# Idle sums moved from the key blocks into the down product, and a second attention with rings of tiles, a bias row by TensorE and another order on each engine

## The chip, the core and the metric

The kernel runs on one core of one Trainium2 chip. The metric is the device time of one execution in microseconds (us), as the median of a few runs.

## What is computed

The input is 32 tiles of 128 tokens with 256 columns. Two layers follow, each an attention over a context and then a feed-forward part, all with residuals:

```
x = x + attention_L0(layernorm(x), ctx, mask)      # 16 heads of 16
x = x + ffn_L0(layernorm(x))                       # 256 -> 768 -> 256, below
x = x + attention_L1(layernorm(x), ctx)            # 16 heads of 64, below
x = x + experts_L1(layernorm(x))                   # 8 experts, 256 -> 1024 -> 256, below

ffn_L0(x):                       # act_qdq rounds to 16 bits; its scale is the maximum of |tensor| over all 32 tiles
  x = act_qdq(x)
  up, gate = act_qdq(x @ dequant(w_up).T), act_qdq(x @ dequant(w_gate).T)
  o = act_qdq(act_qdq(gate * round16(sigmoid(gate))) * up)
  return o @ dequant(w_down).T
attention_L1(q, ctx):
  Q, K, V = q @ Wq + bq, ctx @ Wk + bk, ctx @ Wv + bv
  out = softmax(Q K.T / sqrt(64)) V @ Wo + bo + q
  return layernorm(out) * gamma + beta
experts_L1(x):
  for i in range(8):             # the token's mask is 1 where expert i is its best, else 0
    out += relu((x * mask) @ W1[i] + b1[i]) @ W2[i] + b2[i]
```

For a token that is not an expert's own, the expert still adds relu(b1[i]) @ W2[i] + b2[i], the same row for all tokens. The kernel computes relu(b1) @ W2 once for each expert; these eight rows are the idle sums.

## The kernel before

The program is four functions, one behind the other: attention0, feed_forward0, attention1 and experts. In each, every engine has its own queue of instructions, written out by hand; semaphores tie them. PE is TensorE, DVE VectorE, ACT ScalarE, POOL GpSimd, and SP is SyncE, which issues most of the DMAs; loads of contexts and of weight halves for the key and value blocks are issued on POOL's queue. A number that TensorE needs at more than its rounding is split into a high and a low part, and a product is three matmuls (PARTS). inside(b, first, last) is true where step b lies in that range.

**feed_forward0.** The up and gate products run over 8 chunks of 512 tokens. Then comes the block stage: the 64 key blocks and 64 value blocks of the second attention, 128x512 each, six matmuls a block, which TensorE makes while ScalarE and VectorE do the elementwise part of the FFN, 12 units of 2048 columns. PSUM has seven banks for the blocks and an eighth for the idle sums. ScalarE copies each block out (copy_block), and SP stores it (store_block). ScalarE's queue goes: four blocks; for each unit sigmoid(u) (two passes) and four blocks; copy_idle; three blocks; then, once VectorE and GpSimd have found the scale of the SiLU, quantise_silu for the units with three or four blocks between.

The idle sums are 16 pieces: piece (g, f) takes 128 of the 1024 hidden rows for four experts, as four matmuls of 256 columns onto 32 partitions each. load_w2(i) loads its W2 rows, four DMAs of 128 KB into the one buffer w2, and waits for the piece before to be done. TensorE's queue has idle_sums behind every third block, from the third on. Down stage: 32 tiles, four to a chunk; TensorE makes 18 matmuls of 256 columns a tile (down), ScalarE splits off the high part of the next chunk (high_inner), VectorE adds the residual x1; SP loads x1 and stores x2.

**attention1.** All engines run steps b = FIRST = -4 to LAST = NB + 3 = 35, with Python's unrolled steps at the ends and a hardware loop of four steps between. Step b works on several tiles at once: it turns xn of tile b + 4 (turn_x), projects queries of the pair ahead (queries; from step -2 on), scores and exponentials of tile b in four groups of four heads, half of them in each of two score calls (scores, maxima, exponentials, divide), turns the probabilities (transposes, copy_probT), weights the values (weighted), makes the output product of tile b - 1 (output: 24 matmuls of 256 columns), the output norm of b - 2 (normalise_output), and norm, turning and routing logits of b - 3 and b - 4 (normalise_routed, turn_z, logits_of, route). ps_score (two groups), ps_probT (two), ps_out and ps_proj are PSUM buffers of their own; turned x, turned z, logits and the output product take turns in one bank, ps_aux. Each tile of x2 is loaded twice, into x2_early (four tiles; for xn) and x2_late (four; for the residual and beta). GpSimd makes xn + bo again from x2_late in three passes and x2 + beta in a fourth. Ahead of the first queries TensorE multiplies bv by Wo (bias_through_output, 128 equal rows), which VectorE adds to bo.

The maximum of a group is turned into the bias of the exponential by a second VectorE instruction:

```
dve.tensor_reduce(row_max[:, n, :], ps_score[:, n % 2], AX_X, ALU.max).then_inc(max_done, 1)
dve.wait_ge(max_done, m)
dve.tensor_scalar(shift[:, n, :], row_max[:, n, :], -float(KD) ** -0.5, None, ALU.mult)
...
last = act.activation(prob[:, n, j, :], ps_score[:, n % 2, j, :], ACT.Exp, scale=float(KD) ** -0.5,
                      bias=shift[:, n, j:j + 1], accum_out=row_sum[:, n, j:j + 1])
```

## Time and profile before

| | |
|---|---|
| median of 3 runs | 1651.63 us |
| lowest, highest | 1647.52, 1653.64 us |
| profiled execution, its span | 1649.6 us, 1647.8 us |
| mean granted TensorE clock | 0.92 |
| attention0 | 0 to about 290 us |
| up and gate products | about 290 to 444 us, TensorE busy 140.88 of 154 |
| block stage | 444 to about 701 us |
| down product | about 704 to 775 us |
| end of down, head of attention1 | 775 to 803 us, TensorE busy 12.72 of 28, DMA share 0.72 |
| attention1 | 803 to 1344.8 us |
| experts | 1344.8 to 1647.8 us, TensorE busy 274.92 of 303 |

The span is what the profile shows of the profiled execution, from its first instruction to its last; the execution's own time is 1.8 us longer. An engine's busy time is the sum of its instructions. The granted clock is a share of TensorE's full 2.4 GHz, 0.5 being its lower level of 1.2 GHz. Waiting shows as the gap before an instruction, with the one that ended it.

### The profile page before, as it was taken

What the parts mean: (1) busy time and instruction counts of PE and PEld (TensorE: products, weight loads), DVE (VectorE), ACT (ScalarE), POOL (GpSimd) and SP (SyncE); (2) the same over time, 40 slices, a digit from 0 to 9 for tenths busy, and PEclk for the clock granted to TensorE, in tenths of its full rate; (3) what the DMA queues carried; (4) which work ended last, traced back from release to release, by engine and by line L of the source; (5) the groups of instructions that cost most, each with busy time, mean ns of one, the idle gap of its engine ahead of it and who ended that gap; (6) DMA issues with size and microseconds to landing.
All of it is one profiled execution on the core that took longest, in us unless ns stands there. A gap on an engine that the chain in (4) does not pass through costs nothing. (4 is left out here: it accounts for less than half of the span.)

```text
span 1647.8 us, 35334 instructions
## 1 busy us (share of the span) xinstructions
PE 1389.3 (84%) x11229; PEld 1184.0 (72%) x11229; DVE 1183.1 (72%) x2102; ACT 1047.2 (64%) x2716; POOL 431.9 (26%) x735
## 2 busy tenths in 40 slices
PE   5788888898867689998788888898888867999997
PEld 3455555686744468898677778787777757999996
DVE  6688777887645569086477777777777766888885
ACT  4677778574466656463566666666666625888885
POOL 5444443000000001002123222323232313444443
PEclk9999999899988889999799989989998878999998
DMA  7311010472366778743413232232323135511110
GB/s 225 100 31 35 29 35 28 144 280 90 113 195 199 231 240 268 261 139 109 169 65 114 93 103 77 83 121 76 102 76 120 38 129 210 195 45 54 54 47 9
DMA packets 106773, 194.91 MB, mean 118 GB/s; under 512 B 13474, under 2 KB 72893, under 8 KB 100288
## 3 DMA queue, kind: packets, MB, share of 16 engines
q1 hardware_dynamic: 96320, 160.13, 29.0%
q0 software_dynamic: 10176, 33.57, 6.8%
q8 instruction: 47, 0.77, 0.2%
q14 instruction: 38, 0.31, 0.1%
q10 hardware_dynamic: 192, 0.13, 0.0%
HBM read 128.49 MB, written 68.03 MB: 119 GB/s over the span
## 5 line engine op out<-in xcount | busy, mean ns | idle before, releaser
L1996 ACT ACTIVATE c_w_raw<-c_ps_score,c_shift 128x128 f32<-128x128 f32 x512 | 184.0, 393 | 172.3 <-DVE c_shift L1872 135.9
L2373 PE MATMUL d_ps_hT<-d_zT,d_w_tile 128*128 128x128 f32 x1248 | 148.5, 278 | 1.6 <-DVE d_zT L2480 1.6
L2373 PEld LDWEIGHTS d_ps_hT<-d_zT,d_w_tile 128*128 128x128 f32 x1248 | 145.3, 195 | 2.3 <-DVE d_zT L2480 2.3
L2386 PE MATMUL d_ps_y<-d_w_parts,d_hT 128*128 128x256 f32 x936 | 121.8, 287 | 1.8 <-DVE d_res L2511 1.8
L1996 ACT ACTIVATION_READ_ACCUMULATOR c_w_raw<-c_ps_score,c_shift 128x1 f32 x512 | 118.8, 232 | 0.0
L2386 PEld LDWEIGHTS d_ps_y<-d_w_parts,d_hT 128*128 128x128 f32 x936 | 114.6, 191 | 2.0 <-DVE d_res L2511 2.0
L581 ACT ACTIVATE a_probT<-a_ps_probT 128x512 f32<-128x512 f32 x128 | 71.1, 623 | 66.2 <-PE a_ps_probT L368 66.2
L459 DVE TENSOR_REDUCE a_row_max<-a_ps_score 128x8 f32<-128x1024 f32 x64 | 78.0, 1218 | 48.6 <-PE a_ps_score L357 48.6
L2546 ACT ACTIVATE d_h<-d_ps_hT,d_b1T 128x128 f32<-128x128 f32 x312 | 88.7, 367 | 37.8 <-PE d_ps_hT L2373 37.8
L2499 DVE TENSOR_TENSOR d_w_parts<-d_w,d_w_parts 128x1024 fp32r<-128x1024 f32 x78 | 95.2, 1221 | 23.7 <-ACT d_w_parts L2558 23.7
L1754 PE MATMUL c_ps_proj<-c_xnT,c_wq 128*128 128x256 f32 x768 | 105.9, 288 | 0.0
L1801 PE MATMUL c_ps_aux<-c_wo,c_attnT 128*128 128x256 f32 x768 | 99.3, 285 | 3.0 <-DVE c_attnT L1892 2.9
L1724 PE MATMUL c_ps_score<-c_kT,c_qT 64*128 64x128 f32 x1024 | 92.6, 332 | 8.5 <-ACT c_w_raw L1996 6.9
L1754 PEld LDWEIGHTS c_ps_proj<-c_xnT,c_wq 128*128 128x128 f32 x768 | 94.4, 191 | 3.8 <-issue 0.2
L1801 PEld LDWEIGHTS c_ps_aux<-c_wo,c_attnT 128*128 128x128 f32 x768 | 93.6, 191 | 4.8 <-issue 3.4
L1724 PEld LDWEIGHTS c_ps_score<-c_kT,c_qT 64*128 64x128 f32 x1024 | 79.2, 232 | 24.8 <-ACT c_w_raw L1996 12.7
L1869 DVE TENSOR_REDUCE c_row_max<-c_ps_score 128x4 f32<-128x512 f32 x128 | 87.4, 683 | 7.7 <-PE c_ps_score L1724 7.5
L1699 POOL TENSOR_TENSOR c_var_o<-c_mv_o,c_eps 128x1 f32<-128x1 f32 x32 | 6.8, 213 | 327.0 <-DVE c_mv_o L1915 327.0
L1878 DVE RECIPROCAL c_inv_sum<-c_row_sum 128x4 f32<-128x4 f32 x128 | 22.4, 175 | 97.1 <-ACT c_w_raw L1996 97.1
L1880 DVE TENSOR_TENSOR c_w_raw<-c_w_raw,c_inv_sum 128x512 f32<-128x512 f32 x128 | 88.6, 692 | 4.5 <-DVE c_inv_sum L1878 0.2
L1043 PE MATMUL b_ps<-b_ctx_high,b_w_parts 128*128 128x512 f32 x256 | 91.9, 431 | 0.0
L2558 ACT ACTIVATE d_w_parts<-d_w 128x1024 fp32r x78 | 80.4, 1054 | 13.7 <-PE d_ps_y L2386 12.6
(299 smaller groups left out, 3731.3 us busy)
## 6 DMA issues: line engine op xcount, KB each, us to landing
keys_scratch<-b_out SPq DMA_DIRECT2D x64, 256.0 KB, 3.6
values_scratch<-b_out SPq DMA_DIRECT2D x64, 256.0 KB, 3.6
c_kT<-keys_scratch SPq DMA_DIRECT2D x16, 1024.0 KB, 6.4
d_w<-w_in SPq DMA_DIRECT2D x16, 1024.0 KB, 8.0
split_scratch<-b_split SPq DMA_DIRECT2D x12, 1024.0 KB, 4.7
c_v_more<-values_scratch SPq DMA_DIRECT2D x24, 512.0 KB, 3.9
b_ctx_high<-split_scratch POOLq DMA_DIRECT2D x16, 512.0 KB, 6.1
b_ctx_low<-split_scratch POOLq DMA_DIRECT2D x16, 512.0 KB, 7.5
```

What stands on the lines that cost most here:

```text
L1043: last = pe.matmul(ps[:, bank(n), :], w_parts[:, h, a, k, column:column + P], ctx_parts[c % 2][b][:, k, :], start=(j == 0), stop=(j == ND ...
L1724: last = pe.matmul(ps_score[:, r, j, :], qT[rows, s, blk, tok], kT[rows, s, blk, tok], start=True, stop=True)
L1754: last = pe.matmul(ps_proj[:, j, h * PT:(h + 1) * PT], weights[:, a, k, blk * P:(blk + 1) * P], src[:, c, k, :], start=(n == 0), stop=(n = ...
L1801: last = pe.matmul(ps_aux[:, 0:D], attnT[:, s, a, blk, :], wo[:, c, blk, :], start=(n == 0), stop=(n == BLKS * len(PARTS) - 1))
L1869: dve.tensor_reduce(row_max[:, n, :], ps_score[:, n % 2], AX_X, ALU.max).then_inc(max_done, 1)
L1880: dve.tensor_tensor(prob[:, n], prob[:, n], inv_sum[:, n, :].unsqueeze(2).to_broadcast([P, HB, P]), ALU.mult).then_inc(prob_ready, 1)
L1996: last = act.activation(prob[:, n, j, :], ps_score[:, n % 2, j, :], ACT.Exp, scale=float(KD) ** -0.5, bias=shift[:, n, j:j + 1], accum_out ...
L2373: last = pe.matmul(ps_hT[:, f, :], w1_tile[:, half, k, n * P:(n + 1) * P], zT[:, s, k, :], start=(k == 0), stop=(k == ND - 1))
L2386: last = pe.matmul(ps_y[:, 0:D], hT[:, s, a, f, :], w2_parts[:, half, b, n, :], start=(f == 0 and (a, b) == PARTS[0]), stop=(f == FB - 1 a ...
L2499: dve.tensor_tensor(w2_parts[:, half, 1], w2[:, e, half * FB // 2:(half + 1) * FB // 2, :], w2_parts[:, half, 0].bitcast(F32), ALU.subtrac ...
L2546: act.activation(h[:, f, :], ps_hT[:, f, :], ACT.Relu, bias=b1T[:, e, f:f + 1]).then_inc(h_ready, 1)
L2558: act.activation(w2_parts[:, half, 0], w2[:, e, half * FB // 2:(half + 1) * FB // 2, :], ACT.Copy)\
```

## The change

In feed_forward0 the idle sums leave the block stage: TensorE makes one piece behind every second tile of the down product (odd n; 16 pieces, 32 tiles). w2 becomes a ring of three buffers, with a semaphore each, in memory that yT, upT and gateT held before; SP issues load_w2(t // 2) at even t among its loads of x1 and stores of x2. ScalarE copies the sums out (copy_idle) at the end of its down loop, and they are stored ahead of the last x2. The down product's loops on SP and TensorE are written out.

In attention1 one ring of eight x2 tiles takes the place of two of four, and each tile is loaded once; xn has a ring of eight too and is itself the residual, so that GpSimd only adds beta. bo (with bv Wo) comes in as a matmul of two rows of ones by the two parts of bo, ahead of the output product and into the same bank; bias_through_output makes two rows, in step 0 instead of step -2. The queries are scaled by 1/8 as they are copied (their bias bq ahead of the loop), the maximum is written negated and is itself the exponential's bias. normalise_output has two VectorE passes of two operations instead of three passes. The hardware loop takes eight steps, twice. The order within a step changes on PE, DVE and ACT, and the loads at the head change order. In experts, one small ScalarE activation (at_tile) stands ahead of some copies instead of behind them.

The core of the diff, with sixteen columns of indentation cut. It leaves out names, semaphores, the same edits where they repeat, TensorE's order within a step (shown below), and the new bias_parts, which are five VectorE instructions on two rows of 256 that split bo into its two parts.

```diff
-w2 = x_space[:, 0:4 * D].rearrange("p (e d) -> p e d", d=D)
-idle = x_space[:, 0:BANK].rearrange("p (g d) -> p g d", g=2)
-down_int = x_space[:, BANK:BANK + NF * D // 4].bitcast(I16)
+w2 = [raw_at(f"w2_{n}", [P, 4, D], offset)
+for n, offset in enumerate((address["yT"] + 4 * (2 * T - ITEM), address["upT"], address["gateT"]))]
+idle = out2[:].rearrange("p (g d) -> p g d", g=2)
...
+    if t >= 4:
         sp.wait_ge(x2_ready, t - 3)
     sp.dma_start(x1_sb[:, s, :], x1_dram[t]).then_inc(x1_loaded[s], 16)
-    if inside(t, 3, NB - 1):
+    if t >= 3:
         store(t - 3, (s + 1) % 4)
+    if t % 2 == 0:
+        load_w2(t // 2)
...
-    if i >= 1:
-        sp.wait_ge(idle_part, i)
+    if i >= 3:
+        sp.wait_ge(idle_part, i - 2)
     for e in range(4):
-        sp.dma_start(w2[:, e, :], w2_dram[4 * g + e][:, f, :]).then_inc(w2_loaded, 16)
+        sp.dma_start(w2[i % 3][:, e, :], w2_dram[4 * g + e][:, f, :]).then_inc(w2_loaded[i % 3], 16)
...
-    if n % IDLE_EVERY == IDLE_EVERY - 1 and w2_pieces < 2 * FB:
-        load_w2(w2_pieces)
-        w2_pieces += 1
-    if n == KEYS:
-        sp.wait_ge(idle_ready, 1)
-        for e in range(4):
-            sp.dma_start(idle_dram[e:NE:4].unsqueeze(0), idle[32 * e:32 * e + 1]).then_inc(idle_stored, 16)
 sp.wait_ge(block_done, ALL)
 sp.dma_start(wq_raw[:], wq_dram).then_inc(wq_loaded, 16)
-sp.wait_ge(idle_stored, 64)
...
-for t in range(4):
-    step(t, t)
-with sp.Fori(1, NB // 4) as i:
-    for s in range(4):
-        step(4 * i + s, s)
-for t in range(NB - 3, NB):
-    store(t, t % 4)
+for t in range(NB):
+    step(t, t % 4)
+store(NB - 3, (NB - 3) % 4)
+store(NB - 2, (NB - 2) % 4)
+sp.wait_ge(idle_ready, 1)
+for e in range(4):
+    sp.dma_start(idle_dram[e:NE:4].unsqueeze(0), idle[32 * e:32 * e + 1]).then_inc(idle_stored, 16)
+store(NB - 1, (NB - 1) % 4)
 sp.wait_ge(wq_loaded, 16)
+sp.wait_ge(idle_stored, 64)
...
-    pe.wait_ge(w2_loaded, 64 * (i + 1))
+    pe.wait_ge(w2_loaded[i % 3], 64 * (i // 3 + 1))
...
             pe.wait_ge(x2_ready, n - TILES + 1)
         for j, (f, (a, b)) in enumerate(product(range(NF), PARTS)):
             last = pe.matmul(ps[:, t, 0:D], inner[:, s, a, f, t * P:(t + 1) * P],
                              down_parts[b][:, f, :], start=(j == 0), stop=(j == NF * len(PARTS) - 1))
         last.then_inc(down_done, 1)
-for c in range(2):
-    down(c, c)
-with pe.Fori(1, NC // 2) as i:
-    for s in range(2):
-        down(2 * i + s, s)
+        if n == 1:
+            pe.wait_ge(relu_b1_ready, 1)
+        if n % 2 == 1:
+            idle_sums(n // 2)
+for c in range(NC):
+    down(c, c % 2)
...
-copy_idle()
 copy_blocks(done, done + 3)
 done += 3
...
-pool.wait_ge(bo_added, 1)
-def residuals(t, u, i):
-    s = u % 2
-    pool.wait_ge(late_loaded[u], 16 * uses(t, None if i is None else i + 1))
...
-    pool.tensor_tensor(xn_bo[:, s, :], xn_bo[:, s, :], bo[:], ALU.add).then_inc(xn_bo_ready, 1)
-    pool.tensor_tensor(x2_late[:, u, :], x2_late[:, u, :], beta[:], ALU.add).then_inc(x2_beta_ready, 1)
+pool.wait_ge(bias_loaded, 16 * N_BIAS)
+def residual(t, w):
+    pool.wait_ge(xn_ready, t + 1)
+    pool.tensor_tensor(x2[:, w, :], x2[:, w, :], beta[:], ALU.add).then_inc(x2_beta_ready, 1)
...
+    if inside(b, 4, NB):
+        bank_after_logits(b)
+    else:
         pe.wait_ge(xnT_ready, b + 5)
-    else:
-        bank_after_logits(b)
-    pe.wait_ge(attnT_ready, 2 * t + 2)
     if isinstance(b, int) and b == 1:
         pe.wait_ge(w_split, 2)
+        pe.wait_ge(bo_ready, 1)
+        pe.wait_ge(ones_ready, 1)
+    pe.matmul(ps_aux[:, 0:D], two_ones[:], bo_parts[:], start=True, stop=False)
+    pe.wait_ge(attnT_ready, 2 * t + 2)
...
+def normalise(t, w, uses_now):
+    dve.wait_ge(x2_loaded[w], 16 * uses_now)
+    if inside(t, RING, NB - 1):
+        dve.wait_ge(xnT_done, t - RING + 1)
+        dve.wait_ge(proj_ready, t - RING + 1)
+    dve.tensor_scalar(xn[:, w, :], x2[:, w, :], mv2[:, t, 0:1], rstd2[:, bass.ds(t, 1)],
                       ALU.subtract, ALU.mult).then_inc(xn_ready, 1)
 def maxima(b, n):
-    m = NU * b + n + 1
     dve.wait_ge(scores_done, 2 * b + n // 2 + 1)
-    dve.tensor_reduce(row_max[:, n, :], ps_score[:, n % 2], AX_X, ALU.max).then_inc(max_done, 1)
-    dve.wait_ge(max_done, m)
-    dve.tensor_scalar(shift[:, n, :], row_max[:, n, :], -float(KD) ** -0.5, None, ALU.mult)\
-       .then_inc(shift_ready, 1)
+    dve.tensor_reduce(neg_max[:, n, :], ps_score[:, n % 2], AX_X, ALU.max, negate=True).then_inc(max_done, 1)
...
-    dve.wait_ge(xn_bo_ready, t + 1)
-    dve.tensor_tensor(proj[:, s, :], ps_aux[:, 0:D], xn_bo[:, s, :], ALU.add).then_inc(proj_ready, 1)
+    dve.tensor_tensor(proj[:, s, :], ps_aux[:, 0:D], xn[:, w, :], ALU.add).then_inc(proj_ready, 1)
...
+    dve.wait_ge(mv_o_done, t + 1)
+    dve.scalar_tensor_tensor(proj[:, s, :], proj[:, s, :], mv_o[:, s, 0:1], gamma[:],
+                             ALU.subtract, ALU.mult).then_inc(scaled_done, 1)
     dve.wait_ge(rstd_o_done, t + 1)
-    dve.tensor_scalar(proj[:, s, :], proj[:, s, :], mv_o[:, s, 0:1], rstd_o[:, s, :],
-                      ALU.subtract, ALU.mult).then_inc(normed_done, 1)
-    dve.wait_ge(normed_done, t + 1)
-    dve.tensor_tensor(proj[:, s, :], proj[:, s, :], gamma[:], ALU.mult).then_inc(scaled_done, 1)
     dve.wait_ge(scaled_done, t + 1)
     dve.wait_ge(x2_beta_ready, t + 1)
     if inside(t, 4, NB - 1):
         dve.wait_ge(zx_stored[u], 16 * (uses(t, i) - 1))
-    dve.tensor_tensor(x3[:, u, :], proj[:, s, :], x2_late[:, u, :], ALU.add).then_inc(x3_ready, 1)
+    dve.scalar_tensor_tensor(x3[:, u, :], proj[:, s, :], rstd_o[:, s, :], x2[:, w, :],
+                             ALU.mult, ALU.add).then_inc(x3_ready, 1)
...
-    if isinstance(b, int) and b == projects[0]:
-        dve.wait_ge(bias_loaded, 16 * N_BIAS)
-        dve.wait_ge(bias_turned, 1)
-        dve.tensor_tensor(bo[:], bo[:], ps_out[:, 0:2, :].rearrange("p h k -> p (h k)"), ALU.add).then_inc(bo_added, 1)
-    if inside(b, FIRST, NB - 5):
-        normalise(b + 4, u, None if i is None else i + 2)
     here, back = inside(b, 0, NB - 1), inside(b, 1, NB)
-    if back:
-        split_attn(b - 1, (u + 1) % 2, 0)
+    if not inside(b, 0, LAST) and inside(b, FIRST, NB - 5):
+        normalise(b + 4, (w + 4) % RING, 1)
     if here:
         maxima(b, 0)
         maxima(b, 1)
-    if inside(b, 2, NB + 1):
-        normalise_output(b - 2, (u + 2) % 4, turn[2])
-    if inside(b, 4, NB + 3):
-        route(b - 4)
-    if here:
-        divide(b, 0)
-        divide(b, 1)
+    if back:
+        split_attn(b - 1, (u + 1) % 2, 0)
     if isinstance(b, int) and (b, 0) in split_at:
         rest_of_weights(split_at[b, 0])
     if inside(b, FIRST, NB - 5):
         split_x(b, u)
+    if isinstance(b, int) and (b, 1) in split_at:
+        rest_of_weights(split_at[b, 1])
+    if inside(b, 2, NB + 1):
+        normalise_output(b - 2, (u + 2) % 4, (w - 2) % RING, turn[2])
+    if here:
+        divide(b, 0)
+        divide(b, 1)
+    if back:
+        split_attn(b - 1, (u + 1) % 2, 1)
+    if inside(b, 4, NB + 3):
+        route(b - 4)
     if inside(b, 3, NB + 2):
         normalise_routed(b - 3, (u + 1) % 4, turn[3])
-    if back:
-        split_attn(b - 1, (u + 1) % 2, 1)
-    if isinstance(b, int) and (b, 1) in split_at:
-        rest_of_weights(split_at[b, 1])
     if here:
         maxima(b, 2)
         maxima(b, 3)
+    if isinstance(b, int) and b == 0:
+        bias_parts()
+    if here:
         divide(b, 2)
+    if inside(b, -1, NB - 6):
+        normalise(b + 5, (w + 5) % RING, ring_uses(b, w, i, 5))
+    if back:
+        add_residual(b - 1, (u + 1) % 2, (w - 1) % RING)
+    if here:
         divide(b, 3)
     if back:
-        add_residual(b - 1, (u + 1) % 2)
-    if isinstance(b, int) and (b, 3) in split_at:
-        rest_of_weights(split_at[b, 3])
...
-def step(b, u, i):
+def step(b, w, i):
+    u = w % 4
     if isinstance(b, int) and b == projects[0]:
-        act.wait_ge(bias_loaded, 16 * N_BIAS)
+        act.wait_ge(bq_scaled, 1)
     here, back = inside(b, 0, NB - 1), inside(b, 1, NB)
     if back:
         copy_attn(b - 1, (u + 1) % 2, 0)
+    if inside(b, FIRST, NB - 5):
+        copy_x(b, u)
     if here:
         exponentials(b, 0)
-    if inside(b, 4, NB + 3):
-        copy_z(b - 4)
-    copy_queries(b, u, 0)
     if back:
         copy_probT(b - 1, 2)
         copy_probT(b - 1, 3)
     if here:
         exponentials(b, 1)
-    copy_queries(b, u, 1)
-    if isinstance(b, int) and split_at.get((b, 0)):
-        round_weights(split_at[b, 0])
-    if inside(b, FIRST, NB - 5):
-        copy_x(b, u)
+    if inside(b, 4, NB + 3):
+        copy_z(b - 4)
+    copy_queries(b, u, 0)
     if back:
         copy_attn(b - 1, (u + 1) % 2, 1)
-    if isinstance(b, int) and split_at.get((b, 1)):
-        round_weights(split_at[b, 1])
+    copy_queries(b, u, 1)
     if here:
         exponentials(b, 2)
-    if here:
         copy_probT(b, 0)
         copy_probT(b, 1)
         exponentials(b, 3)
-    if isinstance(b, int) and split_at.get((b, 3)):
-        round_weights(split_at[b, 3])
+    if isinstance(b, int) and (b, 1) in split_at:
+        round_weights(split_at[b, 1])
```

TensorE's queue (PE), one step of attention1's loop, before (names begin with c_, the function's letter; a number behind x counts equal instructions; ps_score is the scores, ps_proj the queries, zx turned into ps_aux is turn_z, xn into ps_aux turn_x, wr the logits, v the weighted sum, wo the output product):

```order
L1724 MATMUL c_ps_score<-c_kT,c_qT 128x128 x8
L1754 MATMUL c_ps_proj<-c_xnT,c_wq 128x256 x12
L1811 MATMUL c_ps_aux<-ident,c_zx 128x128 x2
L1733 MATMUL c_ps_probT<-ident,c_w_raw 128x128 x8
L1754 MATMUL c_ps_proj<-c_xnT,c_wq 128x256 x12
L1776 MATMUL c_ps_aux<-c_wr,c_zT 128x8 x2
L1788 MATMUL c_ps_aux<-ident,c_xn 128x128 x2
L1745 MATMUL c_ps_out<-c_w_raw,c_v_more 64x128 x8
L1724 MATMUL c_ps_score<-c_kT,c_qT 128x128 x8
L1733 MATMUL c_ps_probT<-ident,c_w_raw 128x128 x8
L1801 MATMUL c_ps_aux<-c_wo,c_attnT 128x256 x24
L1745 MATMUL c_ps_out<-c_w_raw,c_v 64x128 x8
```

and the same step after the change:

```order
L1708 MATMUL c_ps_score<-c_kT,c_qT 128x128 x8
L1770 MATMUL c_ps_aux<-ident,c_xn 128x128 x2
L1717 MATMUL c_ps_probT<-ident,c_w_raw 128x128 x8
L1738 MATMUL c_ps_proj<-c_xnT,c_wq 128x256 x12
L1799 MATMUL c_ps_aux<-ident,c_zx 128x128 x2
L1729 MATMUL c_ps_out<-c_w_raw,c_v_more 64x128 x8
L1738 MATMUL c_ps_proj<-c_xnT,c_wq 128x256 x12
L1760 MATMUL c_ps_aux<-c_wr,c_zT 128x8 x2
L1708 MATMUL c_ps_score<-c_kT,c_qT 128x128 x8
L1717 MATMUL c_ps_probT<-ident,c_w_raw 128x128 x8
L1783 MATMUL c_ps_aux<-c_bo_parts,c_two_ones 128x256
L1786 MATMUL c_ps_aux<-c_wo,c_attnT 128x256 x24
```

What moved: the turning of xn and of the rest of the last tile's probabilities now come right behind the first scores, ahead of the queries; the second weighted sum comes ahead of the second queries; turned z comes between the two halves of the queries, and the logits directly ahead of the second scores; the bias row (c_bo_parts) stands ahead of the output product.

TensorE's queue in the block stage before, at one idle sum (b_x_space is the buffer w2, b_b1T relu(b1); w_parts and ctx are the operands of a key block):

```order
L1043 MATMUL b_ps<-b_ctx_high_2913,b_w_parts 128x512 x2
L1043 MATMUL b_ps<-b_ctx_low_2914,b_w_parts 128x512
L1043 MATMUL b_ps<-b_ctx_high_2913,b_w_parts 128x512
L1018 MATMUL b_ps<-b_x_space,b_b1T 32x256 x4
L1043 MATMUL b_ps<-b_ctx_high_2913,b_w_parts 128x512
L1043 MATMUL b_ps<-b_ctx_low_2914,b_w_parts 128x512
L1043 MATMUL b_ps<-b_ctx_high_2913,b_w_parts 128x512 x2
L1043 MATMUL b_ps<-b_ctx_low_2914,b_w_parts 128x512
```

and in the down product after the change, at the same idle sum's new place (b_w_0 is the first buffer of the ring; down_low, down_high and inner are the operands of the down product):

```order
L1076 MATMUL b_ps<-b_down_low,b_inner 128x256
L1076 MATMUL b_ps<-b_down_high,b_inner 128x256
L1011 MATMUL b_ps<-b_w_0_2917,b_b1T 32x256 x4
L1076 MATMUL b_ps<-b_down_high,b_inner 128x256
L1076 MATMUL b_ps<-b_down_low,b_inner 128x256
L1076 MATMUL b_ps<-b_down_high,b_inner 128x256 x2
L1076 MATMUL b_ps<-b_down_low,b_inner 128x256
```

What moved: the four matmuls of the piece stand between two tiles of the down product and no longer between two key blocks.

## Rows read from the trace of the kernel before

**Rows 1.** The page: the span, and each engine's busy time, share and instructions.
```profile
span 1647.8 us, 35334 instructions
...
PE 1389.3 (84%) x11229; PEld 1184.0 (72%) x11229; DVE 1183.1 (72%) x2102; ACT 1047.2 (64%) x2716; POOL 431.9 (26%) x735
```
**Rows 2.** Windows of all engines: busy us (x instructions), granted clock, DMA share, GB/s.
```profile
444.00:701.00 257.00, 208.53 (x910) 156.83 (x908) 136.59 (x93) 150.67 (x171) 19.49 (x35) 0.89 0.73 232
720.00:760.00 40.00, 40.00 (x335) 40.00 (x335) 31.11 (x58) 24.59 (x9) 0.00 (x0) 1.00 0.40 124
...
803.00:1344.80 541.80, 461.71 (x4296) 414.78 (x4296) 397.40 (x954) 345.85 (x1398) 139.97 (x249) 0.91 0.26 83
```
**Rows 3.** Waits in the block stage: the group of TensorE's idle sums.
```profile
PE b_ps L1018 <- DMA b_x_space<-w_in: 43.4, 10, 8.6
```
**Rows 4.** Timeline of ScalarE, block and down stages: start, duration, instruction, wait before it.
```profile
457.42 1.28 ACT L1157 ACT_TABLE_LOAD   x1
...
563.67 1.99 ACT L1157 ACTIVATE b_act<-yT,b_factors 128x2048 f32<-128x2048 int16 x1
...
570.00 1.99 ACT L1157 ACTIVATE b_act<-yT,b_factors 128x2048 f32<-128x2048 int16 x1
...
590.33 3.89 ACT L1164 ACTIVATE yT<-b_act,b_factors 128x2048 int16<-128x2048 f32 x2
...
678.45 0.60 ACT L1175 ACTIVATE b_out<-b_ps 128x512 f32<-128x512 f32 x1 [0.81 <-PE b_ps L1053]
```
**Rows 5.** Timeline of TensorE in attention1, tiles 2, 13 and 28.
```profile
830.76 1.16 PE L1724 MATMUL c_ps_score<-c_kT,c_qT 64*128 64x128 f32 x16 [0.40 <-ACT c_w_raw L1996]
...
1011.02 1.16 PE L1724 MATMUL c_ps_score<-c_kT,c_qT 64*128 64x128 f32 x16
...
1014.61 1.66 PE L1754 MATMUL c_ps_proj<-c_xnT,c_wq 128*128 128x256 f32 x12
...
1017.23 0.61 PE L1776 MATMUL c_ps_aux<-c_wr,c_zT 128*128 128x8 f32 x4 [0.95 <-ACT c_zT L2038]
1018.83 0.44 PE L1788 MATMUL c_ps_aux<-ident,c_xn 128*128 128x128 f32 x2 [0.99 <-DVE logits L1903]
...
1020.90 2.08 PE L1724 MATMUL c_ps_score<-c_kT,c_qT 64*128 64x128 f32 x16
...
1023.76 3.07 PE L1801 MATMUL c_ps_aux<-c_wo,c_attnT 128*128 128x256 f32 x24
...
1026.77 1.09 PE L1745 MATMUL c_ps_out<-c_w_raw,c_v_more 128*64 128x128 f32 x16
1028.06 1.16 PE L1724 MATMUL c_ps_score<-c_kT,c_qT 64*128 64x128 f32 x16 [0.20 <-ACT c_w_raw L1996]
...
1263.83 1.16 PE L1724 MATMUL c_ps_score<-c_kT,c_qT 64*128 64x128 f32 x16 [0.21 <-ACT c_w_raw L1996]
```
**Rows 6.** Windows, a stretch of 3.7 us in attention1.
```profile
1002.30:1006.00 3.70, 3.70 (x34) 3.25 (x33) 2.47 (x6) 2.44 (x10) 0.66 (x1) 0.54 1.02 319
```
**Rows 7.** Timeline of TensorE: an idle sum, and the head of attention1.
```profile
503.29 0.64 PE L1018 MATMUL b_ps<-b_x_space,b_b1T 128*32 128x256 f32 x8
...
783.29 0.69 PE L1788 MATMUL c_ps_aux<-ident,c_xn 128*128 128x128 f32 x2 [8.57 <-DVE c_xn L1863]
...
790.96 5.27 PE L1819 MATMUL c_ps_out<-c_w_raw,c_bv 128*128 128x256 f32 x16 [4.06 <-DMA c_br<-br_in]
```
**Rows 8.** DMA issues of w2: instructions, KB each, median us to landing.
```profile
b_x_space<-w_in SPq DMA_DIRECT2D x64, 128.0 KB, 2.7
```
**Rows 9.** VectorE by line and shape, 850 to 1290 us.
```profile
L1869 DVE TENSOR_REDUCE c_row_max<-c_ps_score 128x4 f32<-128x512 f32 x106 | 72.4, 683 | 6.5 <-PE c_ps_score L1724 6.4
...
L1921 DVE TENSOR_SCALAR c_proj<-c_proj,c_mv_o,c_rstd_o 128x256 f32<-128x256 f32 x27 | 23.9, 886 | 0.0
```
**Rows 10.** Timeline of ScalarE in attention1, around one tile's copies of probabilities.
```profile
1024.04 0.37 ACT L1996 ACTIVATE c_w_raw<-c_ps_score,c_shift 128x128 f32<-128x128 f32 x1 [2.27 <-PE c_ps_probT L1733]
...
1025.42 1.10 ACT L2011 ACTIVATE c_w_raw<-c_ps_probT 128x512 f32<-128x512 f32 x2
```

223 lines of the change are left out of this document (112 added, 111 removed).

## The prediction, made before the changed kernel ran

> **What bounds the kernel now.** I first read the page [rows 1]: no engine is busy all the time (TensorE 84%, VectorE 72%, ScalarE 64%), so waits between engines set the end, and these differ by stage. The span cut into stages [rows 2] shows two in which TensorE, the engine with most to do, is not full: the 128 key and value blocks (444 to 701 us: busy 208.5 of 257 us) and the second attention (803 to 1344.8 us: 461.7 of 541.8 us). In the down product between them it has no gap (40.00 of 40 us).
>
> In the block stage the table of waits [rows 3] says what TensorE waits for: 43.4 us for the w2 pieces of the idle sums. These stand in its queue ahead of the next key block, so ScalarE's copies of key blocks wait behind them, and behind the copies in ScalarE's queue stand the sigmoids that the scale of the SiLU needs. ScalarE's rows [rows 4]: the table load of the first sigmoid is at 457.42 us, quantising the SiLU begins at 590.33 us. Where nothing holds ScalarE up, a unit (two passes over 2048 columns, four block copies) takes 570.00 - 563.67 = 6.33 us. In the later part TensorE gives a block every 0.60 + 0.81 = 1.4 us (the copy and ScalarE's wait for the next).
>
> In the attention I took one tile in TensorE's queue [rows 5], 1011.02 to 1028.06 us: 17.0 us. Tiles 2 and 28 start at 830.76 and 1263.83 us: 26 periods of 16.66 us in the mean. The reader is to see two holes, ahead of the logits (0.95 us, for ScalarE's copy of zT) and of the turning of xn (0.99 us, for VectorE's routing row; all of them use the PSUM bank ps_aux). Then the scores take 2.08 us instead of 1.16 us. At this place of the tile before, the granted clock is 0.54 of full over 3.7 us [rows 6]: mostly the 1.2 GHz level, after two such holes. So the holes cost twice.
>
> **The change, part by part.** The sum is made against the profiled execution's 1649.6 us (span 1647.8 and 1.8 around it), 0.1% under the median of 1651.63 us of the three timed runs.
>
> *Idle sums out of the block stage.* Block 3 no longer waits for w2, so the first sigmoid can start some 7 us earlier, at 450.5 us. Four blocks are 5.6 us of TensorE, under ScalarE's 6.33: ScalarE sets the pace. 12 units x 6.33 = 76 us and about 1 us of table load end at 528 us, the last sigmoid in them at 525 us. Two VectorE passes and the scale behind it are some 6 us by the size of ScalarE's passes. Quantising the SiLU then starts at 531 us instead of 590.33: 59 us earlier. What is behind it (73 blocks, 110 us before) shrinks a little, because TensorE is now up to seven PSUM banks ahead of ScalarE instead of level with it: by 0 if the DMA queues bind there, by 110 - 73 x 1.4 = 8 us and a few of lead, 13 in all, if not. I take 6. Gain 65 (59 to 72).
>
> *Idle sums in the down product.* TensorE has no gap there to hide them, so all 16 count: 16 x 0.6 [rows 7] = 10 us. Each needs 4 x 128 KB, issued on SyncE's queue among the loads of x1 and the stores of x2. Such a load lands in 2.7 us at the median [rows 8], and the ring of three issues piece i four tiles ahead (18 products each; 8.6 us). Nothing more if it lands in time (0); 16 x 2.7 = 43 if every one is waited for whole. I take 0.5, for the first. At the end ScalarE's copy of the idle row (0.6, as a block copy) and four more issues stand ahead of the last store of x2, for which the stage's end waits (8.57 us from TensorE's last product to its next work [rows 7]); the four I take as 2 us, since one such transfer whole is 2.7. Loss 2.5 (0 to 5).
>
> *Head of the attention.* TensorE waited until 790.96 us for the bias rows and spent 5.27 us on the bias through the output weights, ahead of the first queries [rows 7]. Now queries start once three tiles are turned. But VectorE's rest of wo comes just ahead of the first maxima, and the bias product moves into tile 0. Gain 3 (0 to 8).
>
> *A tile of the attention.* In the row 1011.02 to the end of the row 1014.61 TensorE does scores, queries, turned z, turned probabilities and queries without a hole in 5.2 us [rows 5]. With logits 0.5, turned xn 0.4, and a weighted sum 1.05 it has 7.1 us to issue from the first scores to the second in the new order too. One wait stays: the weighted sum needs both probT copies, which now come behind the first exponentials. These start about 2.3 us into the tile (scores 1.16, maximum 0.68 [rows 9], two hand-overs, xT's copy). Four exponentials are 1.38 us and two copies 1.0 [rows 10], so it can start at 4.9 us where TensorE is ready at 4.0: 0.9. Behind the second scores the chain is as before: scores 1.16, maximum 0.68, exponentials 1.38, then 2.64 from the copies to the next scores (1025.42 to 1028.06), hand-overs 0.2: 6.1 us; only the shift drops out. Sum 7.1 + 0.9 + 6.1 = 14.1 us. The old holes are covered: zT is copied at 6.6 us and wanted at 7.5, the routing row is wanted only by the output product at 10. TensorE's own work is 7.1 + 1.1 + 0.8 + 3.07 + 1.05 and one row of bias = 13.2 us, the floor. If the 0.9 us lowers the clock as the two holes do (scores +0.92, weighted sum +0.6), a tile takes 15.6.
> 26 tiles x (16.66 - 14.1) = 67. The first two tiles are about even; the last four and the tail, 80 us before, gain 10 by the same chain. Gain 77. Bounds: 13.4 a tile gives 95, 15.6 gives 38.
>
> *The bias row by TensorE* is one more matmul of 256 columns beside 24 that take 3.07 us: 0.13 x 32 = 4 us, within the 13.2. *Prescaled queries and negative maxima* drop the shift, counted above. *GpSimd* loses three of its four passes over 256 columns a tile; it was busy 140 of 541.8 us [rows 2], so nothing. *VectorE's output norm* has two passes for three. VectorE had 397.4/32 = 12.4 us of work a tile [rows 2] and has under 12 now, below 14.1: 0. *Experts:* one ScalarE copy changes place ahead of work that VectorE finishes later: 0.
>
> Sum: -65 + 10 + 0.5 + 2.5 - 3 - 77 = -132. 1649.6 - 132 = 1517.6, predicted 1518 us.
>
> **The rivals.**
> *Clock still falls in the attention.* The 0.9 us hole takes the place of the old ones: 26 x 1.5 = 39, 1557 us. For it: falls follow holes of 1 us here. Against: there is one, not two within 2 us. Chance 0.2.
> *TensorE is the bound there*, 13.4 a tile: 18 less, 1500 us. It needs the probT copies 0.7 us earlier than I chain them. 0.13.
> *The attention's order gains nothing:* VectorE's last division now stands behind more work and delays the next tile's maxima as its shift did: 1518 + 67 = 1585 us. Against: by my chain VectorE is free 1.4 us after the next scores begin, when it is first wanted. 0.07.
> *VectorE and GpSimd collide.* The first pass of the output norm takes 886 ns in the mean [rows 9] where the same size is 0.4 elsewhere; it is slow when GpSimd adds beta at that moment. If one of the new passes loses 0.48 in every tile, and VectorE is on the chain, 32 x 0.48 = 15: 1533 us. Against: GpSimd's addition comes before them now, and the row is of another kind of pass. 0.06. The Trainium skill speaks for it (SBUF — State Buffer, Who interferes with whom): a VectorE instruction with two SBUF inputs and a GpSimd instruction that reads SBUF exclude each other for the whole instruction, and both new passes are of that kind.
> *The block stage gains nothing,* since DMA bounds it (0.73 busy, 232 GB/s [rows 2]): 1518 + 60 = 1578 us. Against: 0.5 MB for three blocks is no longer moved, and 1.57 MB for four blocks in 6.33 us is 248 GB/s. 0.05.
> *Slower than before.* w2 comes late in the down product: TensorE waits for each of 16 pieces, and the stores of x2 behind them in SyncE's queue are held up too. The gain of 132 us is gone at 132/16 = 8.3 us a piece, near the longest w2 wait (8.6 us) [rows 3]; at 9.5 us each it is 1670 us. Against: the mean of those waits was 4.3, with one buffer and no lead. 0.02.
> My forecast: 0.47.
>
> **How the numbers follow.** The likeliest case has its own range by its terms' bounds: 1503 to 1538. To leave out no more than 2 in 10, the whole range takes in TensorE as the bound with the block gain at its upper bound (1493) and the fallen clock with 5 us of late w2 (1562). A measurement of this kernel tells 0.5% (8 us) from no change. Faster 0.97 (all but the last rival and what is unnamed), same 0.01, slower 0.02.
>
> **What would show it.** Right: no idle sum among the blocks; ScalarE's units 6.3 us apart; SiLU quantising some 59 us earlier; the down product at 80 us instead of 70 with TensorE full; attention tiles 14.1 us apart at the full clock, without a wait for the routing row. Wrong: units above 7 us, or ScalarE waiting for stores of keys; TensorE waiting for w2 in the down product; tiles above 15 us with a low granted clock, or VectorE without a gap.

## The result, and the profile after

The changed kernel takes 1526.26 us (median of 4 runs, 1523.21 to 1530.88) against 1649.72 us for the kernel before beside it: a ratio of 0.925, with a 95% interval of 0.922 to 0.928. Forecast were 1518 us in a range of 1493 to 1562. The profiled execution took 1523.2 us, its span is 1521.4 us; all stages below are of this one, against the profiled one before.

The page after, to stand beside [rows 1]: TensorE works 35 us less in all and fills 89% of the span, where it filled 84%.
```profile
span 1521.4 us, 34563 instructions
...
PE 1354.5 (89%) x11261; PEld 1154.8 (76%) x11261; DVE 1127.4 (74%) x1948; ACT 1046.9 (69%) x2716; POOL 374.4 (25%) x639
```

The stages, each from one mark in TensorE's queue to the next:

| from / to | before | after | change | forecast |
|---|---|---|---|---|
| start to the last gate product | 444.0 | 444.9 | +0.9 | 0 |
| to the first down product | 259.9 | 194.8 | -65.1 | -65 |
| down product with its idle sums | 70.8 | 82.8 | +12.0 | +10.5 |
| to the first turned xn | 8.6 | 9.0 | +0.4 | +2.5 |
| to the scores of tile 2 | 47.5 | 44.7 | -2.7 | -3 |
| scores of tile 2 to those of tile 28 | 433.1 | 367.8 | -65.3 | -67 |
| to the first matmul of experts | 83.5 | 79.8 | -3.7 | -10 |
| experts | 300.5 | 297.6 | -2.8 | 0 |

They sum to -126.4, the difference of the two spans; -132 was forecast.

ScalarE's timeline in the block stage after, to stand beside [rows 4]:
```profile
451.52 1.28 ACT L1145 ACT_TABLE_LOAD   x1
...
515.09 2.02 ACT L1145 ACTIVATE b_act<-yT,b_factors 128x2048 f32<-128x2048 int16 x1
...
521.24 2.02 ACT L1145 ACTIVATE b_act<-yT,b_factors 128x2048 f32<-128x2048 int16 x1
...
531.55 3.90 ACT L1152 ACTIVATE yT<-b_act,b_factors 128x2048 int16<-128x2048 f32 x2 [2.04 <-DVE b_factors L1253]
```

The first sigmoid comes at 451.52 us, two units are 521.24 - 515.09 = 6.15 us apart, and quantising the SiLU begins at 531.55 us, 58.8 us earlier. 451 us, 6.33 us and 59 us were forecast.

TensorE's timeline in and behind the down product:
```profile
639.66 0.35 PE L1076 MATMUL b_ps<-b_down_high,b_inner 128*128 128x256 f32 x1 [3.26 <-DVE b_inner L1446]
...
645.61 0.64 PE L1011 MATMUL b_ps<-b_w,b_b1T 128*32 128x256 f32 x8
646.18 0.39 PE L1076 MATMUL b_ps<-b_down_high,b_inner 128*128 128x256 f32 x1
646.40 0.28 PE L1076 MATMUL b_ps<-b_down_low,b_inner 128*128 128x256 f32 x1
...
650.48 0.28 PE L1076 MATMUL b_ps<-b_down_high,b_inner 128*128 128x256 f32 x1
650.69 0.64 PE L1011 MATMUL b_ps<-b_w,b_b1T 128*32 128x256 f32 x8
...
721.81 0.64 PE L1011 MATMUL b_ps<-b_w,b_b1T 128*32 128x256 f32 x8
731.43 0.69 PE L1770 MATMUL c_ps_aux<-ident,c_xn 128*128 128x128 f32 x2 [8.99 <-DVE c_xn L1856]
```

The pieces stand exactly 5.08 us apart from the first to the last, (721.81 - 645.61)/15: no piece waited for w2. But two tiles took 4.32 us before, so a piece costs 0.76 us.

One tile of the attention after, in TensorE's queue, to stand beside [rows 5]:
```profile
873.26 1.16 PE L1708 MATMUL c_ps_score<-c_kT,c_qT 64*128 64x128 f32 x16
...
876.92 0.39 PE L1799 MATMUL c_ps_aux<-ident,c_zx 128*128 128x128 f32 x2
877.88 1.09 PE L1729 MATMUL c_ps_out<-c_w_raw,c_v 128*64 128x128 f32 x16 [0.58 <-ACT c_w_raw L2016]
878.91 1.66 PE L1738 MATMUL c_ps_proj<-c_xnT,c_wq 128*128 128x256 f32 x12
880.40 0.51 PE L1760 MATMUL c_ps_aux<-c_wr,c_zT 128*128 128x8 f32 x4
880.84 1.16 PE L1708 MATMUL c_ps_score<-c_kT,c_qT 64*128 64x128 f32 x16
...
882.96 0.38 PE L1783 MATMUL c_ps_aux<-c_bo_parts,c_two_ones 2*128 2x256 f32 x1
883.26 3.12 PE L1786 MATMUL c_ps_aux<-c_wo,c_attnT 128*128 128x256 f32 x24
886.31 1.09 PE L1729 MATMUL c_ps_out<-c_w_raw,c_v_more 128*64 128x128 f32 x16
887.34 1.16 PE L1708 MATMUL c_ps_score<-c_kT,c_qT 64*128 64x128 f32 x16
```

From 873.26 to 887.34 us are 14.08 us. There is one hole only, of 0.58 us ahead of the weighted sum, for ScalarE's copies of the last tile's turned probabilities (L2016). From the second scores (880.84) to the next first scores TensorE has no hole at all: 6.50 us. The granted clock there is full, in windows of all engines (busy us by engine, clock, DMA share, GB/s), to stand beside [rows 2]:
```profile
444.00:639.60 195.60, 185.43 (x786) 147.43 (x784) 139.79 (x98) 150.45 (x175) 20.50 (x35) 0.98 0.82 265
640.00:720.00 80.00, 80.00 (x682) 71.78 (x681) 55.04 (x100) 35.99 (x14) 8.78 (x4) 0.98 0.70 217
...
776.00:957.00 181.00, 173.91 (x1765) 157.22 (x1761) 136.59 (x321) 142.54 (x570) 32.69 (x65) 1.00 0.32 105
974.66:978.00 3.34, 3.34 (x25) 3.12 (x25) 1.65 (x3) 0.96 (x5) 0.00 (x0) 0.58 0.02 5
```

The last row is of the one place in the loop where the clock falls clearly: behind TensorE's longest hole there, at the jump back of the loop of eight steps. The tile with the hole takes 16.92 us and the next 14.98, together 3.7 us more than two of 14.08.
```profile
974.66 1.65 PE L1708 MATMUL c_ps_score<-c_kT,c_qT 64*128 64x128 f32 x16 [2.77 <-issue]
```

### The profile page after: what moved, and what is told of

It is laid out like the page before. It is cut to its first block and busy times, and to the rows that moved or that the text cites. A ratio compares the mean times of both kernels' runs of the same rounds, so it can differ in the third digit from the quotient of the medians.

```text
span 1521.4 us, 34563 instructions
## 1 busy us (share of the span) xinstructions
PE 1354.5 (89%) x11261; PEld 1154.8 (76%) x11261; DVE 1127.4 (74%) x1948; ACT 1046.9 (69%) x2716; POOL 374.4 (25%) x639
## 5 line engine op out<-in xcount | busy, mean ns | idle before, releaser
L2001 ACT ACTIVATE c_w_raw<-c_ps_score,c_neg_max 128x128 f32<-128x128 f32 x512 | 183.4, 388 | 51.5 <-DVE c_neg_max L1861 50.7
L2001 ACT ACTIVATION_READ_ACCUMULATOR c_w_raw<-c_ps_score,c_neg_max 128x1 f32 x512 | 116.0, 227 | 0.0
L1861 DVE TENSOR_REDUCE c_neg_max<-c_ps_score 128x4 f32<-128x512 f32 x128 | 82.5, 686 | 22.9 <-PE c_ps_score L1708 22.9
L1103 ACT ACTIVATE b_act<-b_ps 128x512 f32<-128x512 f32 (+1 forms) x96 | 54.9, 602 | 51.3 <-PE b_ps L988 44.1
L1046 PE MATMUL b_ps<-b_w_parts,b_ctx_high 128*128 128x512 f32 x256 | 82.0, 402 | 4.1 <-DMA b_ctx_low<-split_scratch 4.1
L1036 PE MATMUL b_ps<-b_ctx_high,b_w_parts 128*128 128x512 f32 x256 | 82.5, 397 | 2.9 <-ACT b_out L1161 2.8
L569 ACT ACTIVATE a_prob<-a_ps_score,a_shift 128x128 f32<-128x128 f32 x256 | 75.4, 413 | 11.5 <-DVE a_shift L463 10.2
```

The lines of the kernel that those rows point to most:

```text
L1036: last = pe.matmul(ps[:, bank(n), :], w_parts[:, h, a, k, column:column + P], ctx_parts[c % 2][b][:, k, :], start=(j == 0), stop=(j == ND ...
L1046: last = pe.matmul(ps[:, bank(n), :], ctx_parts[c % 2][a][:, k, t * P:(t + 1) * P], w_parts[:, h, b, k, :], start=(j == 0), stop=(j == ND ...
L1861: dve.tensor_reduce(neg_max[:, n, :], ps_score[:, n % 2], AX_X, ALU.max, negate=True).then_inc(max_done, 1)
```

## The experiments

Twelve kernels ran. Where spans are compared, each is that of the run's profiled execution.

### One part alone

Two kernels take one function of the change each: feed_forward0, or attention1, the rest being that of before.

```diff
 # ffn_part                      # attn_part
+def feed_forward0 (changed)      def feed_forward0 (before)
 def attention1 (before)         +def attention1 (changed)
 def experts (before)             def experts (before)
```

> The kernel before with the new feed_forward0 alone; attention1 and experts are those of before. Theory (the terms add up): the stretch from 444 us to the first down product shortens by 64 us as in the changed kernel, the down product lengthens by 12 (16 pieces at 0.76 us), its end by about 0.4: 1649.6 - 64 + 12.4 = 1598 us, and attention1 has its old tile of 16.7 us. Rival (the parts need each other: the old head of attention1 loads x2 twice and now has four idle stores ahead of it): the gap between down product and scores grows by 5 us or more: 1603 us or above.

> The kernel before with the new attention1 alone. Theory (the terms add up): from the first turned xn to the start of experts 74.5 us less, as in the changed kernel, nothing elsewhere: 1649.6 - 74.5 = 1575 us, tile 14.1 us at a granted clock of 0.98. Rival (part of the attention's gain comes from the state the new down product leaves, its clock above all): tile over 14.5 us, 1585 us or more.

Measured: ffn_part 1594.56 us, ratio to before 0.966 (0.962 to 0.970); attn_part 1584.20 us, 0.958 (0.954 to 0.962). The two ratios take off 3.4% and 4.2%, together 7.6% where the whole change takes off 7.5%: the parts add up. In ffn_part the first down product starts 194.9 us behind the last gate product, where the changed kernel has 194.8, and the attention's tile is 16.65 us; the gap to the first turned xn is 8.1 us, so its rival (5 us more there) is out. attn_part came out 9 us above its 1575 in the median, and 14 us in its profiled execution (1589.05). From the first turned xn to experts it took 493.0 us, as the changed kernel's 492.3, and its tile is 14.13 us in the mean: the attention gained in full. Most of the 14 us lies in the parts that it shares with before: its block stage took 266.5 us instead of 259.9 and its experts 302.2 instead of 300.5. Another 3 us were my sum's: the 74.5 us that I had taken for the attention hold the 2.8 us of experts, and without them the changed kernel gains 71.7 there. So the old block stage can differ by 6.6 us from one execution to the next, which bears on the next section.

### What the block stage gained: the wait, the bytes, or the matmuls

Two kernels start from the one before. In w2_no_wait all of w2 is loaded as before, but TensorE does not wait for it; SyncE, which issues the loads and the stores of blocks in one queue, waits for each piece's landing before it issues the next. In w2_once only the first piece is loaded. TensorE makes all 16 pieces at their old places in both. The idle rows are others than the reference's in both.

```diff
 # w2_no_wait: load_w2, idle_sums
-sp.wait_ge(idle_part, i)
+sp.wait_ge(w2_loaded, 64 * i)
-pe.wait_ge(w2_loaded, 64 * (i + 1))
-    b1T[...].to_broadcast([P, 32]), w2[:, e, :],
+    b1T[...].to_broadcast([P, 32]), w_parts[:, 0, 0, e % 2, 0:D].bitcast(F32),
 # w2_once: SyncE's loop over the blocks, idle_sums
-if n % IDLE_EVERY == IDLE_EVERY - 1 and w2_pieces < 2 * FB:
-    load_w2(w2_pieces)
-    w2_pieces += 1
-pe.wait_ge(w2_loaded, 64 * (i + 1))
+pe.wait_ge(w2_loaded, 64)
```

> The kernel before with nobody waiting for w2: the 16 pieces are loaded as before (64 loads of 128 KB, one piece after the other has landed), and TensorE makes its 16 idle sums at the same places, but from the rows of the key weights that are there already, so the idle rows are others than the reference's. Theory (the gain in the block stage is that of the wait, through ScalarE's queue): from 444 us to the first down product about 195 us as in the changed kernel and 3 to 10 more for the 16 x 0.64 us of matmuls that stay, 198 to 205 against 260 before: 1590 us. Rival (the bytes, 8.4 MB more through DMA queues that are 0.82 busy without them, are what costs): 220 us or more.

> The kernel before with the first w2 piece alone loaded: 15 of 16 loads (7.9 MB) are left out, all 16 idle sums use the rows of the first, and nobody waits after the first, so the idle rows are others than the reference's. It splits the 25 us that remained between the run w2_no_wait (220 us from 444 us to the first down product) and the changed kernel (195). Theory (the bytes delay the stores of blocks, for which ScalarE waits): about 200 us here, the matmuls costing 5 and the bytes 20. Rival (TensorE's 10 us and ScalarE's lost lead cost most of it): 212 us or more.

Measured: 1608.20 us, ratio 0.977 (0.972 to 0.981), and 1600.55 us, 0.971 (0.968 to 0.974). From the last gate product to the first down product w2_no_wait took 665.39 - 445.3 = 220.1 us and w2_once 653.35 - 443.2 = 210.2, where the kernel before took 259.9 and the changed one 194.8. My theory said 198 to 205 for the first, and its rival 220 or more. So TensorE's wait for w2 was only some 40 of the 65 us (some, because the old stage alone took 259.9 and 266.5 us in two executions). Without it, ScalarE waited for the stores of blocks. The table of waits (engine, tile, line, for what: us in total, times, longest) of w2_no_wait, from 444 to 660 us, and ScalarE's first sigmoid:
```profile
ACT b_out L1172 <- DMA keys_scratch<-b_out: 27.7, 10, 5.1
...
ACT b_out L1174 <- DMA values_scratch<-b_out: 19.7, 11, 3.5
```
```profile
452.76 1.28 ACT L1156 ACT_TABLE_LOAD   x1
```

the same of w2_once:
```profile
ACT b_out L1172 <- DMA values_scratch<-b_out: 17.8, 11, 3.8
...
ACT b_out L1170 <- DMA keys_scratch<-b_out: 14.0, 7, 4.0
```
```profile
457.48 1.28 ACT L1154 ACT_TABLE_LOAD   x1
```

and the same waits of the changed kernel:
```profile
ACT b_out L1163 <- DMA values_scratch<-b_out: 16.0, 10, 2.6
...
ACT b_out L1161 <- DMA keys_scratch<-b_out: 8.0, 4, 4.4
```

That is 47.4, 31.8 and 24.0 us of waiting for stores; the kernel before had 17.3 of it up to 705 us.

w2_once still waits for its first piece: counted from the last gate product, its first sigmoid comes at 457.48 - 443.19 = 14.3 us, that of the changed kernel at 451.52 - 444.89 = 6.6. This is 7.7 of the 210.2 - 194.8 = 15.4 us between them, and I had forgotten it. The other 7.7 us are the 16 pieces, for which I had expected 5, with whatever else sets the two apart: ScalarE waits 7.8 us longer for stores in w2_once, and the runs don't separate the two.

w2_no_wait has the pieces too and only 0.8 us of the first wait (452.76 - 445.33 = 7.4), so 220.1 - 194.8 - 7.7 - 0.8 = 17 us go with its 15 more pieces of w2, 7.9 MB. I had called this the price of the bytes. The traces say something else. SyncE's own waits in w2_no_wait, and the stores of key blocks in both runs (KB each, median us from issue to landing), w2_no_wait first:
```profile
SPq L846 <- DMA b_x_space<-w_in: 32.1, 14, 4.7
```
```profile
keys_scratch<-b_out SPq DMA_DIRECT2D x64, 256.0 KB, 5.1
```
```profile
keys_scratch<-b_out SPq DMA_DIRECT2D x64, 256.0 KB, 5.0
```

A store takes as long from its issue to its landing with the 7.9 MB as without (in the changed kernel 3.3 us; why it is less there is open). But SyncE stood 32.1 us for pieces of w2 to land, a wait that my edit had put there, with the stores of blocks behind it in its queue. So the 17 us are those of the loads' place in SyncE's queue, as far as the traces tell, and not of full DMA queues; loads from another queue were not tried. Of the 65 us TensorE's wait gave some 40, the loads of w2 in SyncE's queue about 17, and the pieces with what is left about 8.

### Order or operations

old_order is the changed kernel with the old orders within a step on TensorE, VectorE and ScalarE, and the waits for the bank ps_aux that go with them; everything else of it stays. old_order_shift adds the shift.

```diff
 # TensorE, old_order (VectorE and ScalarE in the same way)
     scores(b, u, 0, i)
-    turn_x(b, w)
-    transposes(b - 1, 2); transposes(b - 1, 3)
     queries(b, u, 0)
     turn_z(b, u)
-    weighted(b - 1, (u - 1) % 4, 1)
+    transposes(b - 1, 2); transposes(b - 1, 3)
     queries(b, u, 1)
     logits_of(b - 4)
+    turn_x(b, w)
+    weighted(b - 1, (u - 1) % 4, 1)
     scores(b, u, 1, i)
 # old_order_shift also
-dve.tensor_reduce(neg_max[:, n, :], ps_score[:, n % 2], AX_X, ALU.max, negate=True).then_inc(max_done, 1)
+dve.tensor_reduce(row_max[:, n, :], ps_score[:, n % 2], AX_X, ALU.max).then_inc(row_done, 1)
+dve.wait_ge(row_done, m)
+dve.tensor_scalar(neg_max[:, n, :], row_max[:, n, :], -1.0, None, ALU.mult).then_inc(max_done, 1)
```

> The changed kernel with the orders of before within a step on TensorE, VectorE and ScalarE (and the waits for the bank ps_aux that go with them); all its new operations, rings, loads and its loop of eight steps stay. Theory (the order covers the two holes at ps_aux, and the holes cost twice by the clock; the operations only save the shift): a tile near 16.2 us with a granted clock of about 0.91, holes ahead of the logits and of the turned xn: 1521 + 27 x 2.1 = 1580 us. Rival (fewer and shorter VectorE and GpSimd passes made the gain): a tile of 14.1 to 14.6 us whatever the order, 1521 to 1535 us.

> The kernel of the run old_order with the maximum's sign turned by a VectorE instruction of its own again, four a tile, ahead of each group's exponentials. It splits the 0.98 us a tile that the new operations gave in the old order. Theory (the shift is on the chain twice a tile, once for each score call, at about 0.2 us, and the longer holes lower the clock now and then): tile 16.1 us, 1572 us on the profile. Rival (the shorter output norm on VectorE made the difference): tile 15.7 us, 1561 us.

Measured: old_order 1566.13 us, 0.950 (0.947 to 0.954), span 1560.4; old_order_shift 1578.70 us, 0.958 (0.955 to 0.962). The mean tile from the scores of tile 2 to those of tile 28 is 16.66 us before, 16.10 with the shift, 15.68 without it, and 14.15 with the new order. So with the new operations in place the order gives 1.53 us; with the old order the shift gives 0.42, and 0.55 comes from the rest of the new operations and buffers, which no run takes apart. I had given the old order 16.2 us: it falls between theory and rival. TensorE's queue in old_order:
```profile
919.35 0.61 PE L1760 MATMUL c_ps_aux<-c_wr,c_zT 128*128 128x8 f32 x4 [0.41 <-ACT c_zT L2038]
920.40 0.43 PE L1772 MATMUL c_ps_aux<-ident,c_xn 128*128 128x128 f32 x2 [0.44 <-DVE logits L1890]
921.13 1.49 PE L1729 MATMUL c_ps_out<-c_w_raw,c_v_more 128*64 128x128 f32 x16 [0.29 <-ACT c_w_raw L2011]
922.55 2.08 PE L1708 MATMUL c_ps_score<-c_kT,c_qT 64*128 64x128 f32 x16
```

The two old holes at ps_aux are there, but at 0.41 and 0.44 us for 0.95 and 0.99 in [rows 5]. A likely reason, argued and not shown, is that VectorE comes to the routing row sooner. Its output norm has two passes of 474 and 484 ns (VectorE by line and shape, changed kernel):
```profile
L1915 DVE SCALAR_TENSOR_TENSOR c_zx<-c_proj,c_rstd_o,c_x 128x256 f32<-128x256 f32 x25 | 12.1, 484 | 2.9 <-issue 1.2
L1908 DVE SCALAR_TENSOR_TENSOR c_proj<-c_proj,c_mv_o,c_gamma 128x256 f32<-128x256 f32 x25 | 11.9, 474 | 0.0
```

where one of the three passes of before alone took 886 ns [rows 9]. The number of passes is not all of it, since the passes of before were slow beside GpSimd. Here is the second of them (L1924, two inputs in SBUF) in two tiles of the kernel before, with GpSimd's addition of beta in the first:
```profile
866.55 0.78 POOL L1695 TENSOR_TENSOR c_x_late<-c_x_late,c_beta 128x256 f32<-128x256 f32 x1
```
```profile
866.77 0.83 DVE L1924 TENSOR_TENSOR c_proj<-c_proj,c_gamma 128x256 f32<-128x256 f32 x1
...
931.59 0.42 DVE L1924 TENSOR_TENSOR c_proj<-c_proj,c_gamma 128x256 f32<-128x256 f32 x1
```

It takes 0.83 us where it overlaps with that addition, in 10 of 32 tiles, and 0.42 to 0.43 in the other 22. The pass ahead of it (L1921) overlaps with GpSimd's passes over 256 columns in 30 tiles, at 0.89 us in the mean, and takes 0.41 in the two where it does not. My prediction had set the operations down as the shift alone.

### How long a hole the clock bears

long_hole and longer_hole make the changed kernel's one hole longer, by cutting ScalarE's copies of the probabilities in pieces.

```diff
-    copy_probT(b - 1, 2)
-    copy_probT(b - 1, 3)
+    copy_probT(b - 1, 2)       # longer_hole: copy_probT(b - 1, 2, 4)
+    copy_probT(b - 1, 3, 4)    # four activations of 128 columns for one of 512
```

> The changed kernel with one of ScalarE's two copies of the last tile's probabilities made in four pieces of 128 columns, so that TensorE's hole ahead of the weighted sum grows from 0.58 us to about 1.1. This is my rival that the clock still falls, made on purpose. Theory (one hole of 1 us in a tile leaves the clock at full): tile 14.6 us, granted clock 0.98 in the loop, 1521 + 30 x 0.5 = 1536 us. Rival (a hole of 1 us lowers the clock, as two did before): clock 0.93 or less, matmuls of the first scores or behind them at twice their time in many tiles, tile 15.5 us or more, 1560 us.

> The kernel of the run long_hole with both copies of the last tile's probabilities in four pieces each, since one grew the hole only from 0.58 to 0.77 us. The hole should be 0.96 us, as long as each of the two in the old order. Theory (one such hole in a tile leaves the clock at full): tile 14.45 us, granted clock 0.98 or more in the loop, 1533 us on the profile. Rival (it lowers the clock): clock 0.95 or less in the loop, tile 15 us or more, 1550 us.

Measured: 1533.62 us, 0.931 (0.928 to 0.934), and 1537.68 us, 0.932 (0.929 to 0.936). The first was too weak a test: its hole was 0.77 us, not 1.1. The second has what was wanted, in TensorE's queue and in windows of the loop:
```profile
868.63 1.09 PE L1729 MATMUL c_ps_out<-c_w_raw,c_v_more 128*64 128x128 f32 x16 [0.95 <-ACT c_w_raw L2018]
```
```profile
803.00:957.00 154.00, 144.21 (x1469) 130.64 (x1467) 114.39 (x270) 122.10 (x541) 27.63 (x55) 1.00 0.30 97
975.00:1144.00 169.00, 157.03 (x1567) 142.38 (x1567) 120.91 (x285) 129.56 (x569) 27.52 (x56) 0.98 0.31 103
```

One hole of 0.95 us in each tile, and the clock stays at or by full; the tile is 14.46 us, which is 14.08 + 0.95 - 0.58. The rival that the clock still falls is out. It fell behind a longer idle stretch or behind several: it is 0.54 behind the old two holes [rows 6], it falls in some tiles of old_order (matmuls of 1.49 and 2.08 us behind its three short holes; 0.63 from 922.5 to 926 us) and not in others with nearly the same holes (1.00 from 905 to 908 us, behind 0.33, 0.44 and 0.29 us), and it is 0.58 behind the hole of 2.77 us at the loop's jump (window above).

### Taking away what bounds the tile now

By the rows above a tile is TensorE's own work (13.5 us) and the hole of 0.58. probT_first takes the hole away, bias_pool takes the bias row off TensorE, both is the two together, and all_three also writes the steps out.

```diff
 # probT_first, ScalarE
-    exponentials(b, 0)
     copy_probT(b - 1, 2)
     copy_probT(b - 1, 3)
+    exponentials(b, 0)
 # bias_pool: GpSimd, TensorE, VectorE
+    pool.tensor_tensor(xn_bo[:, w % 2, :], xn[:, w, :], bo[:], ALU.add).then_inc(xn_bo_ready, 1)
-    pe.matmul(ps_aux[:, 0:D], two_ones[:], bo_parts[:], start=True, stop=False)
-    dve.tensor_tensor(proj[:, s, :], ps_aux[:, 0:D], xn[:, w, :], ALU.add).then_inc(proj_ready, 1)
+    dve.wait_ge(xn_bo_ready, t + 1)
+    dve.tensor_tensor(proj[:, s, :], ps_aux[:, 0:D], xn_bo[:, s, :], ALU.add).then_inc(proj_ready, 1)
 # all_three
-with engine.Fori(1, NB // RING - 1) as i:
...
+for b in range(first, last + 1):
+    step(b, b % RING, None)
```

> The changed kernel with one swap in ScalarE's queue: both copies of the last tile's probabilities ahead of the first exponentials. Theory (a tile is TensorE's own 13.5 us plus a hole of 0.58 us for these copies): the hole goes, tile 13.5 us, 30 tiles x 0.58 = 17 us less than the changed kernel: 1509 us. Rival (the exponentials are on the chain, as my prediction summed it): they come 1.1 us later, and with them the divisions, the second pair of transposes or the copy of zT ahead of the logits, so that a hole of the same size stands there: 1526 us or more.

> The changed kernel with the bias row taken off TensorE: GpSimd adds bo (128 equal rows again) to xn in one pass of its own, and VectorE adds that to the output product. Theory (TensorE sets the second part of a tile, 6.50 us from the second scores to the next first scores): the row's matmul of 0.30 us drops out of every tile, 31 x 0.30 = 9 us less than the changed kernel, 1517 us, tile 13.8. Rival (the chain scores, maximum, exponentials, copies sets it at 6.4 to 6.5 us, and TensorE only just keeps up): 0 to 3 us less, 1524 us; if VectorE waits for GpSimd, more than the changed kernel.

> The changed kernel with both edits of the first round that paid: the copies of the last tile's probabilities ahead of the first exponentials, and the bias row by GpSimd. Theory (TensorE alone sets the tile): 13.42 - 0.30 = 13.1 us a tile, 27 us less than the changed kernel, 1495 us on the profile. Rival (without its slack the second part is set by the chain of scores, maximum, exponentials and copies): 13.3 to 13.4 us a tile, 1502 us.

> The kernel of the run both with attention1's 40 steps written out, without the loop of eight. Theory (the jump back of the loop leaves TensorE without instructions for 2.8 us, and its clock is low behind it): the two long tiles go, 15.85 + 14.50 - 2 x 13.13 = 4.1 us less than the run both, 1490 us. Rival (straight code has to be fetched as well, 8 steps more of it on each engine, or the hole is no matter of the jump): no gain, or a loss, 1494 us or more.

| kernel | median us | ratio to before (95%) | span us | mean tile us |
|---|---|---|---|---|
| changed kernel | 1526.26 | 0.925 (0.922 to 0.928) | 1521.4 | 14.15 |
| probT_first | 1504.78 | 0.911 (0.908 to 0.914) | 1503.6 | 13.55 |
| bias_pool | 1511.96 | 0.915 (0.912 to 0.918) | 1510.1 | 13.83 |
| both | 1494.18 | 0.906 (0.903 to 0.909) | 1494.6 | 13.25 |
| all_three | 1489.70 | 0.904 (0.901 to 0.907) | 1487.8 | 13.05 |

All four tiles went by theory; the times of probT_first and bias_pool came out 4 and 5 us under the 1509 and 1517 that I had summed. TensorE's queue in probT_first, from first scores to the next, without a hole:
```profile
867.01 1.16 PE L1708 MATMUL c_ps_score<-c_kT,c_qT 64*128 64x128 f32 x16
...
870.67 0.39 PE L1799 MATMUL c_ps_aux<-ident,c_zx 128*128 128x128 f32 x2
870.98 1.09 PE L1729 MATMUL c_ps_out<-c_w_raw,c_v 128*64 128x128 f32 x16
...
873.93 1.16 PE L1708 MATMUL c_ps_score<-c_kT,c_qT 64*128 64x128 f32 x16
...
880.43 0.83 PE L1708 MATMUL c_ps_score<-c_kT,c_qT 64*128 64x128 f32 x10
```

That is 13.42 us, and 6.50 from the second scores as before: exponentials that start 1.1 us later delay nobody. In bias_pool it is 0.32 us a tile less, the row's matmul, and GpSimd's pass does not delay TensorE. In both the two add up, to 13.04 to 13.22 us a tile away from the jump. In all_three the two long tiles at the jump are gone, 13.14 and 13.04 us for 15.85 and 14.50; at the place of the jump TensorE goes on from the weighted sum to the scores of tile 16:
```profile
956.56 1.09 PE L1724 MATMUL c_ps_out<-c_w_raw,c_v_more 128*64 128x128 f32 x16
957.76 1.16 PE L1703 MATMUL c_ps_score<-c_kT,c_qT 64*128 64x128 f32 x16
```

The stretch from tile 2 to tile 28 is 5.2 us shorter than in both (339.4 for 344.6), but the ratios' intervals overlap, so the gain is shown in the trace and not by the times. all_three is the fastest kernel here: 9.6% under the kernel before and 2.4% under the changed one (1489.7 of 1526.3 us).

## Why the prediction was right, by its steps

**What bounds the kernel.** Right. The two stages named as not full gave 65.1 us and, the attention's head and tail with it, 71.7, of which the down product took 12 back. The chain w2, next key block, ScalarE's copies, sigmoids is shown by w2_no_wait: with TensorE's wait gone, quantising the SiLU begins at 556.5 us instead of 590.3.

**Block stage, -65.** Right in size (-65.1), and the steps behind it measured nearly as they were put: first sigmoid at 451.5, units 6.15 for 6.33 us, SiLU 58.8 earlier. The cause I gave was only part of it. The text has the w2 wait as the whole gain and its rival "DMA bounds it" at a gain of nothing. The runs split the 65 into some 40 for TensorE's wait, about 17 for the loads of w2, which no longer stand in SyncE's queue ahead of stores of blocks, and about 8 for the pieces with what is left. The sum came out because it was built from ScalarE's pace when nothing holds it up [rows 4], which holds whatever had held it up. In this it was lucky: read as a forecast of "make w2 arrive in time, but leave it there", it would have been 25 us too high.

**Idle sums in the down product, +10 and +0.5.** The mechanism was right, the term mis-sized: +12.0. No piece waited for w2, so the 0.5 that I took for the first was nothing. Up to the next down product a piece takes 0.57 us (645.61 to 646.18), near the 0.6 that I took. The other 0.19 are at its two seams: the product behind a piece has 0.22 us to itself (646.18 to 646.40) and the one ahead of the next piece 0.21 (650.48 to 650.69), where such products follow each other every 0.12 us. The tiles themselves run as before.

**Stage end, +2.5.** +0.4: the four idle stores are issued ahead of the last x2 store, but the gap hardly grew. The bound of nothing was the right value.

**Head of the attention, -3.** -2.7 up to the scores of tile 2, by a long tile 0 (17.5 us, with the bias product and the exponential's table in it) behind a shorter start, as put.

**A tile, 14.1.** It measured 14.08 in the loop, 14.15 in the mean of 26, yet errors of opposite sign cancel in it, which is luck. The hole is 0.58 us, not 0.9. And the second part of the tile is not the chain of 6.1 us through ScalarE but TensorE's own work without a gap, 6.50 us: I had put TensorE's work at 13.2 us a tile, it is 13.5, of which the bias row is 0.30 (882.96 to 883.26) where I had 0.13. So that row was not free "within the 13.2": bias_pool shows 0.32 us a tile for it. What I wrote as the bound, 13.4 for "TensorE is the bound there", is what probT_first then runs at, 13.42, for the reason given there, the copies coming earlier.

**The operations.** "Only the shift drops out", and VectorE's shorter output norm counted 0: by old_order and old_order_shift the operations gave 0.98 us in the old order, 0.42 of it the shift. This term was put at too little, though for the new order its size stays open. There TensorE sets the tile, and how much of the 0.98 is needed was not tried.

**The tail, -10.** -3.7. The last tiles gained less: before, they already ran at 14.7 to 15.8 us, since their steps hold less work, and I had used the chain of a full step for them. **Experts, 0.** -2.8. The five profiled executions with the experts of before took 298.8 to 302.2 us there (mean 300.4), the nine with the changed ones 297.6 to 299.0 (298.1). So executions differ by as much, but some 2 us may belong to the one activation that changed place; it was not tried alone.

**The rivals.** Clock still falls: out, longer_hole. Attention's order gains nothing: out, 1.53 us a tile by old_order. VectorE and GpSimd collide: the Trainium skill (SBUF — State Buffer, Who interferes with whom) has a VectorE pass with two SBUF inputs contend with a GpSimd instruction that reads SBUF. Both new passes are of that kind, and run at 474 and 484 ns in the mean, where 256 columns in other passes take 0.40 to 0.43. In the changed kernel they do not meet GpSimd's addition of beta, so nothing is lost. The trace of before agrees with the page: its pass of this kind took 0.83 us beside GpSimd's addition and 0.42 without it. The w2 pieces late in the down product: out, they stand 5.08 us apart.

## What to carry to other kernels

An estimate built from the pace of the engine behind the wait can be right while its cause is not: before the wait alone is mended, one should ask what else goes with the moved work, here loads in a queue shared with stores, and matmuls, which made 25 of the 65 us. Once the holes of a stage are closed, the engine that was waiting has become the bound, and every instruction that the change added to it (the bias row) costs its full time from then on: move such work back to an engine with slack. And where the busiest engine has one hole left, look at what its releaser does just before: exchanging two groups of instructions in ScalarE's queue took 1.4% off.

## What the runs showed of the hardware

- One idle stretch of 0.95 us in every 14.46 us leaves TensorE's clock at full (1.00 and 0.98 granted); two of 0.95 and 0.99 us within 2 us brought it to 0.54, mostly the lower level of 1.2 GHz.
- A loop's jump back is not free where its body is long: with eight steps TensorE stood 2.77 us without anything that it waited for, and its clock fell to 0.58 behind it, 3.7 us in all. In the kernel before, with four steps in the loop, TensorE's queue shows no idle time of this kind in the attention. Written out, the steps ran through, with no hole at that place. The Trainium skill (Runtime: NRT & Kernel Launch, Instruction fetch mechanics) says that TensorE's instruction memory holds 2048 instructions. It also says that a taken branch to a target outside the current window of two pages has to wait for a fetch. The trace agrees if TensorE's window is the 2048: 776 to 957 us is 12.9 tiles with 1765 matmuls and 1761 weight loads, so 8 steps are some 2190 instructions, and 4 steps 1100. If the window were the 512 instructions that the page gives for most engines' memories, the loop of four steps would have waited too, and it did not. That the hole is such a fetch is argued by these counts; that it goes with the loop is shown. I had not weighed this rule, which spoke against the longer loop; it cost 3.7 us.
- Loads in the queue of other transfers slowed these: in w2_no_wait SyncE stood 32.1 us for pieces of w2 to land, and ScalarE waited 47.4 us for stores of blocks, instead of 31.8 in w2_once, though a store of keys took 5.1 and 5.0 us at the median from its issue in the two.
- A VectorE pass with two inputs in SBUF took 0.83 us where GpSimd added beta beside it, and 0.42 where it did not (L1924 in the kernel before).
- An activation of 512 columns cut in four costs little: the hole behind it grew by 0.19 us for each copy that was cut.
